# A rotation whose halves are exchanged by transfers of the sine term instead of by a second set of products

## The chip, the core and the metric

The kernel runs on one core of one Trainium2 chip. The metric is the device time of one execution in microseconds (us). Three runs of the kernel before gave a median of 2217.9 us (2217.04 to 2220.73).

## The reference

The program is two transformer layers over 2048 tokens of width 128, in f32. The change lies in the first attention: 16 heads of 64 dimensions, queries and keys made from a latent of 64, and a rotation of all 64 dimensions by the token's place. Cut to what matters:

```python
c_q = h @ w_down_q.T;  c_kv = h @ w_down_kv.T
q = (c_q @ w_up_q.T)  # 16 heads x 64;  k, v from c_kv in the same way
e, o = xr[..., 0::2], xr[..., 1::2]            # even and odd dimensions
rot = stack([e * cos - o * sin, e * sin + o * cos])   # for q and for k
scores = einsum('bhqd,bhkd->bhqk', q, k) / 8
out = softmax(scores) @ v;  out @ w_out.T + residual
```

The first experts, a second attention and second experts follow; the change does not touch them.

## The kernel before

Everything is written out by hand: each engine has its own list of work, sorted by a due time counted in steps, and semaphores join the lists. The function is `heads`. One head has four chunks of 512 queries, one chunk has eight steps of two key tiles, so there are 32 steps to a head and 512 in all.

In a step TensorE (PE) makes two tiles of scores (two 512-column products each, L640 and L641), ScalarE (ACT) writes each tile's exponential twice (f16 at L476, f32 at L477), GpSimd (POOL) subtracts the two for the low half (L428, `low_half`), and PE weighs the values of the step four before with 24 short products (L655 to L659). Between these PE fills the three `aux` banks in PSUM for side work, in the order of `aux_units`: two products a step for the row maxima (L608), which VectorE (DVE) reduces (L533); the shift, the output turn and product; and the rotations.

A rotation ("rope") serves one head's q or k for a pair of chunks, with two chunks on the two halves of the 128 partitions. Each takes two aux units. The first has three products with the weight's columns in even-odd order (`wq`, `wk` and their low halves), the second three with the columns exchanged (`wq_sw`, `wk_sw`). DVE multiplies the first by the cosine (L519), the second by the sine in its bank (L522), and adds the two into `roped` (L527). ACT rounds that to f16 (L464), POOL subtracts for the low half (L422), and SyncE (SP) moves both into the operands: four transfers of the high half (L407), then two of the low half (L413), rotation by rotation. There are 64 rotations: four a head, made during the head before; the first head's stand ahead of the loop, but for its second q rotation, which stands at step 0.

Row maxima of a chunk need the q and k operands in place: the first product for a chunk waits for the high half of q, and those of each key pair for the high and the low half of k. A list's order is fixed, so a wait on one engine holds back everything behind it on that engine.

Ahead of the loop ACT and POOL also split the weights of the later heads (L483 and L435, one instruction per weight on each).

Of the kernel before, what the change touches and what calls it, by code (L numbers as in the profile page):

```python
# [17 lines left out]
P = 128  # L18
# [103 lines left out]

WEIGHTS = ("wq", "wq_sw", "wk", "wk_sw")
FIRST_HEADS = 2 * P
# [175 lines left out]
AUX = 3  # L300
ROPED = 3
STAGED = 2
QRING = 6
PAIRS = NCH // 2
HIGH_MOVES, LOW_MOVES = 4, 2
WEIGHTS_AT = -19
# [4 lines left out]
def rope_at(kind, h, pair):  # L311

    if kind == "k":
        return STEPS * h - (21, 15)[pair] if h else -24 + pair
    return STEPS * h - (27, 5)[pair] if h else (-25, 0)[pair]


def aux_units():

    plan = [(FOLD_AT + 2 * i, "fold", i) for i in range(2)]  # L320
    for h in range(H0):
        for c in range(NCH):
            g, end = NCH * h + c, KPAIR * (NCH * h + c + 1) + LAG
            for kind in "kq" if c % 2 == 0 else "":
                plan += [(rope_at(kind, h, c // 2), "rope", (kind, h, c // 2, part)) for part in range(2)]
# [15 lines left out]
def heads(nc, dram, x, keep):  # L341
    with ExitStack() as ctx:
# [8 lines left out]
        probs_lo = sb("probs_lo", [P, SLOTS, 2, CH], F16)  # L351
        term = [sb(f"rope_term{i}", [P, CH], F32) for i in range(2)]
        roped = [sb(f"roped{i}", [P, CH], F32) for i in range(ROPED)]
        high = [sb(f"rope_high{i}", [P, CH], F16) for i in range(STAGED)]
# [8 lines left out]
        aux = [ps(f"aux{i}", [P, CH], F32) for i in range(AUX)]  # L363
        (aux_full, aux_free, rope_turned, hi_ready, lo_ready, shift_ready, scores_ready, probs_ready, low_ready,
         probs_used, inv_ready, norm_ready, weight_high, weight_ready, xa_full, x_ready) = (
            sem(n) for n in ("aux_full", "aux_free", "rope_turned", "hi_ready", "lo_ready", "shift_ready",
                             "scores_ready", "probs_ready", "low_ready", "probs_used",
                             "inv_ready", "norm_ready", "weight_high",
                             "weight_ready", "xa_full", "x_ready"))
        high_in, low_in = ([sem(f"{n}{i}") for i in range(STAGED)] for n in ("rope_high_in", "rope_low_in"))  # L370
        ident, ident16 = keep["ident"], keep["ident16"]
# [3 lines left out]
        unit_no = {w: n for n, w in enumerate(banked)}  # L375
        ropes = [arg[:3] for kind, arg in banked if kind == "rope" and arg[3] == 0]
        rope_no = {r: n for n, r in enumerate(ropes)}

        def halves_of(kind, h, pair, m):

            c = 2 * pair + m
            if kind == "k":
                a, b, cols = ka[h % 2], kb[h % 2], slice(c * CH, (c + 1) * CH)
            else:
                a, b, cols = qa[(NCH * h + c) % QRING], qb[(NCH * h + c) % QRING], slice(0, CH)
            return a[0:LAT0, cols], a[LAT0:, cols], b[0:LAT0, cols]

        def wait_high(eng, r):
# [7 lines left out]
        with nc.Block() as block:  # L396
            @block.sync
            def _(sp):
                for r, (kind, h, pair) in enumerate(ropes):
                    if r >= STAGED:  # L400
                        wait_high(sp, r - STAGED)
                    sp.wait_ge(hi_ready, r + 1)
                    for m in range(2):
                        a_top, a_bottom, b = halves_of(kind, h, pair, m)
                        rows = high[r % STAGED][m * LAT0:(m + 1) * LAT0, :]
                        for out in (b if kind == "k" else a_top, a_bottom):
                            sp.dma_start(out, rows).then_inc(high_in[r % STAGED], 16)  # L407
                    if r >= STAGED:
                        wait_low(sp, r - STAGED)
                    sp.wait_ge(lo_ready, r + 1)  # L410
                    for m in range(2):
                        a_top, a_bottom, b = halves_of(kind, h, pair, m)
                        sp.dma_start(a_top if kind == "k" else b, low[r % STAGED][m * LAT0:(m + 1) * LAT0, :]  # L413
                                     ).then_inc(low_in[r % STAGED], 16)

            @block.gpsimd
            def _(pool):
                def rope_low(r):
                    pool.wait_ge(hi_ready, r + 1)
                    if r >= STAGED:  # L420
                        wait_low(pool, r - STAGED)
                    pool.tensor_tensor(low[r % STAGED][:], roped[r % ROPED][:], high[r % STAGED][:], ALU.subtract  # L422
                                       ).then_inc(lo_ready, 1)
# [18 lines left out]

                work = [(math.floor(rope_at(*rope)) + 3.5, "rope", r) for r, rope in enumerate(ropes)]
                work += [(n + 1, "low", n) for n in range(ALL)]
# [13 lines left out]
            def _(act):  # L458
                def high_halves(r):
                    act.wait_ge(aux_free, unit_no["rope", (*ropes[r], 1)] + 1)  # L460
# [3 lines left out]
                    act.activation(high[r % STAGED][:], roped[r % ROPED][:], ACT.Copy).then_inc(hi_ready, 1)  # L464

# [26 lines left out]

                work = [(math.floor(rope_at(*rope)) + 2.5, "rope", r) for r, rope in enumerate(ropes)]
                work += [(n, "exp", n) for n in range(ALL)]
# [13 lines left out]
            def _(dve):  # L508
                def empty(kind, arg):
# [4 lines left out]
                    if kind == "rope":  # L514
                        of, h, pair, part = arg
                        r = rope_no[of, h, pair]
                        cols = slice(pair * CH, (pair + 1) * CH)
                        if part == 0:
                            dve.tensor_tensor(term[r % 2][:], bank, keep["cos"][:, cols], ALU.mult  # L519
                                              ).then_inc(aux_free, 1)  # L520
                        else:
                            dve.tensor_tensor(bank, bank, keep["sin"][:, cols], ALU.mult).then_inc(rope_turned, 1)  # L522
                            if r >= ROPED:
                                dve.wait_ge(lo_ready, r - ROPED + 1)
                            dve.wait_ge(aux_free, unit_no["rope", (of, h, pair, 0)] + 1)
                            dve.wait_ge(rope_turned, r + 1)
# [37 lines left out]
                work = [(at, 0, kind, arg) for at, kind, arg in units]  # L564
                work += [(KPAIR * g - 4.9, 1, "reduce", g) for g in range(H0 * NCH)]
                for _, _, kind, arg in sorted(work, key=lambda w: w[:2]):
                    if kind == "reduce":
                        negated_maxima(arg)
                    elif kind == "norm":
                        normalise(arg)  # L570
# [4 lines left out]
            def _(pe):  # L575
                def fill(kind, arg):
# [5 lines left out]
                    if kind == "rope":  # L582
                        of, h, pair, part = arg
                        w = ("wq", "wq_sw", "wk", "wk_sw")[2 * (of == "k") + part]
                        columns, cols = slice(h * P, (h + 1) * P), slice(pair * CH, (pair + 1) * CH)
# [1750 lines left out]
def tables():  # L2336
# [10 lines left out]
    t["cos0"] = by_pair(np.tile(cos, (2, 1)))  # L2347
    t["sin0"] = by_pair(np.concatenate([-sin, sin], 0))

# [32 lines left out]
def layouts(a):  # L2382

    even_odd = np.concatenate([np.arange(0, DH0, 2), np.arange(1, DH0, 2)])
    odd_even = np.concatenate([np.arange(1, DH0, 2), np.arange(0, DH0, 2)])
    twice = lambda w, axis: np.concatenate([w, w], axis)

    def up(w, order):
# [11 lines left out]
        "wq": up(a["L0_attn_w_up_q"], even_odd),  # L2400
        "wq_sw": up(a["L0_attn_w_up_q"], odd_even),
        "wk": up(a["L0_attn_w_up_k"], even_odd),
        "wk_sw": up(a["L0_attn_w_up_k"], odd_even),
        "w_up_v": a["L0_attn_w_up_v"].reshape(H0 // 2, P, LAT0).transpose(1, 0, 2).reshape(P, H0 // 2 * LAT0),
# [48 lines left out]
```

## Time and profile before

| | |
|---|---|
| profiled execution, its own time | 2218.36 us |
| its span, first to last instruction | 2216.5 us |
| mean granted clock of TensorE | 0.935 |
| PE, DVE, ACT, POOL busy in the span | 91%, 76%, 73%, 74% |
| first attention | to about 1260 us of the span |
| transfers, share of 16 engines | 9.2% on the hardware queue |

A busy PE is one whose modelled matmuls overlap, so its share says little of what is left; whether it waits is read from the waits. DVE's and POOL's shares are averages over stages with different limits, and the tables by stretch tell them apart. The attention's loop runs from about 62 us to 1260 us; before it lies a stretch in which the first rotations pass through all engines one after another.

### The profile page before, as it was taken

The numbers are of one execution on the slowest core, as the hardware profiler recorded it, in microseconds if no ns is written. First come the engines' busy times: TensorE is split into PE (matmuls) and PEld (weight loads), VectorE is DVE, ScalarE is ACT, GpSimd is POOL, SyncE is SP. The second block draws the span as 40 slices with busy tenths as digits, with TensorE's granted clock in tenths as the row PEclk, the third lists the DMA queues.
The fourth block names the chain that finished last, engine by engine and source line by source line (L and its number), as shares of the span: only waits on it lengthen the run. The fifth ranks groups of instructions, "written<-read, shape, count | busy, mean of one in ns | idle before, by whom it ended". The sixth has DMA issues, their size and how long they took to land. (4 is left out here: it accounts for less than half of the span.)

```text
span 2216.5 us, 60603 instructions
## 1 busy us (share of the span) xinstructions
PE 2013.8 (91%) x24318; PEld 1318.0 (59%) x24318; DVE 1690.3 (76%) x3487; ACT 1622.9 (73%) x3282; POOL 1630.5 (74%) x1036
## 2 busy tenths in 40 slices
PE   5899999999999999999999989976788887788888
PEld 2466666666666666666666656642456666565665
DVE  5677777777777777777777468968989998899514
ACT  4788898888988989889889846656656565565443
POOL 3699999999999999999999926625663344677600
PEclk8899999999999999999999989978779999998768
DMA  4000100000000000001000001111121111121101
GB/s 152 20 19 23 27 20 23 24 23 23 23 23 23 23 23 23 23 19 28 24 22 18 2 19 27 33 45 26 36 51 36 35 43 38 33 45 39 39 10 38
DMA packets 88224, 67.80 MB, mean 31 GB/s; under 512 B 41280, under 2 KB 78352, under 8 KB 87952
## 3 DMA queue, kind: packets, MB, share of 16 engines
q1 hardware_dynamic: 76432, 52.19, 9.2%
q0 software_dynamic: 11520, 11.82, 2.7%
q8 instruction: 191, 3.13, 0.6%
q14 instruction: 81, 0.66, 0.1%
HBM read 32.97 MB, written 1.61 MB: 16 GB/s over the span
## 5 line engine op out<-in xcount | busy, mean ns | idle before, releaser
L428 POOL TENSOR_TENSOR probs_lo<-probs,probs_hi 128x1024 f16<-128x1024 f32 x512 | 1076.5, 2131 | 65.3 <-ACT probs L477 62.7
L533 DVE TENSOR_REDUCE part_max<-aux 128x1 f32<-128x512 f32 x1024 | 687.8, 687 | 185.6 <-PE aux L608 180.7
L476 ACT ACTIVATE probs_hi<-scores 128x512 f16<-128x512 f32 x1024 | 643.6, 628 | 143.3 <-PE scores L641 116.0
L477 ACT ACTIVATE probs<-scores 128x512 f32<-128x512 f32 x1024 | 649.7, 635 | 0.0
L1732 POOL DMA_INDIRECT far<-key_table,placeT x320 | 326.0, 1019 | 238.3 <-issue 68.6
L655 PE MATMUL acc<-v,probs_hi 128*128 128x65 f16 x4096 | 446.7, 193 | 1.8 <-POOL probs_lo L428 1.8
L657 PE MATMUL acc<-v,probs_hi 128*128 128x64 f16 x4096 | 447.5, 195 | 0.0
L659 PE MATMUL acc<-v,probs_lo 128*128 128x65 f16 x4096 | 445.8, 192 | 0.0
L655 PEld LDWEIGHTS acc<-v,probs_hi 128*128 128x128 f16 x4096 | 382.4, 97 | 73.8 <-POOL probs_lo L428 2.0
L657 PEld LDWEIGHTS acc<-v,probs_hi 128*128 128x128 f16 x4096 | 380.3, 97 | 68.8 <-issue 0.3
L608 PE MATMUL aux<-k_a,q_a 128*128 128x512 f16 x1024 | 393.3, 385 | 13.8 <-DMA k_a<-rope_low 8.5
L640 PE MATMUL scores<-q_a,k_a 128*128 128x512 f16 x1024 | 389.2, 380 | 4.8 <-ACT probs L477 4.7
L641 PE MATMUL scores<-q_b,k_b 65*128 65x512 f16 x1024 | 390.5, 381 | 0.0
L659 PEld LDWEIGHTS acc<-v,probs_lo 128*128 128x128 f16 x4096 | 381.6, 99 | 0.0
L641 PEld LDWEIGHTS scores<-q_b,k_b 65*128 65x128 f16 x1024 | 100.2, 98 | 119.2 <-issue 1.1
L608 PEld LDWEIGHTS aux<-k_a,q_a 128*128 128x128 f16 x1024 | 100.2, 98 | 84.3 <-issue 14.4
L640 PEld LDWEIGHTS scores<-q_a,k_a 128*128 128x128 f16 x1024 | 100.3, 98 | 71.9 <-ACT probs L477 11.8
L1983 PE MATMUL a_turn<-queries,qi 128*128 128x64 f16 x2216 | 83.9, 203 | 40.1 <-DVE qi L1904 39.7
L890 POOL TENSOR_TENSOR e_hid_lo<-e_hid,e_hid_hi 128x512 f16<-128x512 f32 x64 | 74.2, 1160 | 61.4 <-ACT e_hid_hi L842 61.4
L1983 PEld LDWEIGHTS a_turn<-queries,qi 128*128 128x128 f16 x2216 | 79.5, 104 | 46.4 <-issue 41.0
L1757 ACT ACTIVATE far<-a_turn 128x256 f32<-128x256 f32 x34 | 13.0, 383 | 119.3 <-PE a_turn L1983 119.3
L1904 DVE TENSOR_SCALAR qi<-queries,key_id 128x512 f16<-128x512 f16 x277 | 81.5, 363 | 19.8 <-PE a_turn L1983 15.9
(335 smaller groups left out, 3642.0 us busy)
## 6 DMA issues: line engine op xcount, KB each, us to landing
q_a<-rope_high SPq DMA_DIRECT2D x128, 64.0 KB, 2.1
far<-key_table,placeT POOLq DMA_INDIRECT x360, 2.4
q_b<-rope_low SPq DMA_DIRECT2D x64, 64.0 KB, 2.0
k_b<-rope_high SPq DMA_DIRECT2D x64, 64.0 KB, 2.0
k_a<-rope_high SPq DMA_DIRECT2D x64, 64.0 KB, 2.1
k_a<-rope_low SPq DMA_DIRECT2D x64, 64.0 KB, 2.0
qT<-qT SPq DMA_DIRECT2D x16, 256.0 KB
queries<-places SPq DMA_DIRECT2D x7, 512.0 KB, 3.8
```

Source lines behind the costliest of these rows:

```text
L428: pool.tensor_tensor(probs_lo[:, slot], probs[:, wide], probs_hi[:, slot], ALU.subtract).then_inc(low_ready, 1)
L476: act.activation(probs_hi[:, slot, i], bank, ACT.Exp, scale=float(DH0) ** -0.5)
L477: act.activation(probs[:, wide, i], bank, ACT.Exp, scale=float(DH0) ** -0.5).then_inc(probs_ready, 1)
L533: dve.tensor_reduce(part_max[g % 2][:, n % QT, n // QT:n // QT + 1], bank, AX.X, ALU.max).then_inc(aux_free, 1)
L608: ins = pe.matmul(bank, qa[g % QRING][:, t * P:(t + 1) * P], ka[h % 2][:, c * CH:(c + 1) * CH], start=True, stop=True)
L640: pe.matmul(out, ka[h % 2][:, keys], qa[g % QRING][:], start=True, stop=False)
L641: pe.matmul(out, kb[h % 2][:, keys], qb[g % QRING][:], start=False, stop=True).then_inc(scores_ready, 1)
L655: pe.matmul(out, probs_hi[:, n % SLOTS, i, queries], high, start=(kt == 0 and t == 0), stop=False, skip_group_check=True)
L657: pe.matmul(out[:, 0:DH0], probs_hi[:, n % SLOTS, i, queries], low, start=False, stop=False, skip_group_check=True)
L659: ins = pe.matmul(out, probs_lo[:, n % SLOTS, i, queries], high, start=False, stop=(kt == KT0 - 1), skip_group_check=True)
L1732: pool.indirect_dma_start(far[m][:, i, :], None, keep["table"], bass.IndirectOffsetOnAxis(ap=place_of(placeT, t, i), axis=0)).then_inc(far ...
L1983: ins = pe.matmul(b[:, i * KW:(i + 1) * KW], hot_tile(t, k, kt)[:, i * P:(i + 1) * P], split[:, kt, part * KW:(part + 1) * KW], start=(kt ...
```

## The change

The second set of products goes. From one bank DVE makes two products in SBUF, `turned` = bank x sine and `term` = bank x cosine. SP copies the four 32-row halves of `turned` crosswise into `swapped`, and DVE later adds `swapped` to `term` (`join`). The sine table's signs are exchanged to fit. ACT and POOL read `term` where they read `roped`. SP's list is now sorted by due time, with swaps, high moves and low moves of different rotations interleaved. All due times of the rotations are new, and the first head's second q rotation stands ahead of the loop. The two exchanged weights are no longer loaded or split.

```diff
-WEIGHTS = ("wq", "wq_sw", "wk", "wk_sw")
+WEIGHTS = ("wq", "wk")
-ROPED = 3
+TERMS = 4
+HALF0 = LAT0 // 2
+SWAPS, HIGH_MOVES, LOW_MOVES = 4, 4, 2
+JOIN_AFTER, HIGH_AFTER, LOW_AFTER = 3.5, 4.5, 5.5
 def rope_at(kind, h, pair):
     if kind == "k":
-        return STEPS * h - (21, 15)[pair] if h else -24 + pair
-    return STEPS * h - (27, 5)[pair] if h else (-25, 0)[pair]
+        return STEPS * h - (23, 18)[pair] if h else (-26, -25.4)[pair]
+    return STEPS * h - (29, 7)[pair] if h else (-25.7, -20)[pair]
...
+                def swap_halves(r):
+                    sp.wait_ge(aux_free, unit_no["rope", ropes[r]] + 1)
+                    if r >= STAGED:
+                        wait_swapped(sp, r - STAGED)
+                    if r >= TERMS:
+                        sp.wait_ge(roped_ready, r - TERMS + 1)
+                    for m in range(2):
+                        for part in range(2):
+                            src = m * LAT0 + part * HALF0
+                            dst = m * LAT0 + (1 - part) * HALF0
+                            sp.dma_start(swapped[r % TERMS][dst:dst + HALF0, :], turned[r % TERMS][src:src + HALF0, :]
+                                         ).then_inc(swap_in[r % STAGED], 16)
...
+                work = [(rope_at(*rope) + 1, swap_halves, r) for r, rope in enumerate(ropes)]
+                work += [(rope_at(*rope) + HIGH_AFTER + 0.5, move_high, r) for r, rope in enumerate(ropes)]
+                work += [(rope_at(*rope) + LOW_AFTER + 0.5, move_low, r) for r, rope in enumerate(ropes)]
+                for _, move, r in sorted(work, key=lambda w: w[0]):
+                    move(r)
...
-                            dve.tensor_tensor(term[r % 2][:], bank, keep["cos"][:, cols], ALU.mult
-                                              ).then_inc(aux_free, 1)
...
-                            dve.tensor_tensor(bank, bank, keep["sin"][:, cols], ALU.mult).then_inc(rope_turned, 1)
...
-                            dve.tensor_tensor(roped[r % ROPED][:], bank, term[r % 2][:], ALU.add
-                                              ).then_inc(aux_free, 1)
+                        dve.tensor_tensor(turned[r % TERMS][:], bank, keep["sin"][:, cols], ALU.mult)
+                        dve.tensor_tensor(term[r % TERMS][:], bank, keep["cos"][:, cols], ALU.mult).then_inc(aux_free, 1)
...
+                def join(r):
+                    out = term[r % TERMS][:]
+                    dve.wait_ge(aux_free, unit_no["rope", ropes[r]] + 1)
+                    wait_swapped(dve, r)
+                    dve.tensor_tensor(out, out, swapped[r % TERMS][:], ALU.add).then_inc(roped_ready, 1)
```

SP's list at the start, before: each rotation's four high moves and two low moves stand together (`rope_high`, `rope_low` are the staged halves, `q_a`, `q_b`, `k_a`, `k_b` the operands).

```order
L407 DMA q_a<-rope_high 64x512 x4
L413 DMA q_b<-rope_low 64x512 x2
L407 DMA k_b<-rope_high 64x512
L407 DMA k_a<-rope_high 64x512
L407 DMA k_b<-rope_high 64x512
L407 DMA k_a<-rope_high 64x512
L413 DMA k_a<-rope_low 64x512 x2
```

The same list now, from the first swap to the fourth (buffer numbers shown).

```order
L418 DMA rope_swapped0<-rope_turned0 32x512 x4
L418 DMA rope_swapped1<-rope_turned1 32x512 x4
L418 DMA rope_swapped2<-rope_turned2 32x512 x4
L431 DMA k_b0<-rope_high0 64x512
...
L431 DMA q_a1<-rope_high1 64x512 x2
...
L431 DMA k_a0<-rope_high0 64x512
L441 DMA k_a0<-rope_low0 64x512 x2
L441 DMA q_b0<-rope_low1 64x512
L441 DMA q_b1<-rope_low1 64x512
L441 DMA k_a0<-rope_low0 64x512 x2
L418 DMA rope_swapped3<-rope_turned3 32x512 x4
```

The first low move, third in its own rotation before, now stands behind three swaps and three sets of high moves, and the fourth swap behind three sets of low moves.

DVE's list at the start, before: the third rotation, then the first row maxima.

```order
L519 TENSOR_TENSOR rope_term0<-aux1,cos 128x512
L522 TENSOR_TENSOR aux2<-aux2,sin 128x512
L527 TENSOR_TENSOR roped2<-aux2,rope_term0 128x512
L533 TENSOR_REDUCE part_max0<-aux0 128x1
```

DVE's list at the same place now, from the second rotation's cosine on.

```order
L554 TENSOR_TENSOR rope_term1<-aux1,cos 128x512
L553 TENSOR_TENSOR rope_turned2<-aux2,sin 128x512
L554 TENSOR_TENSOR rope_term2<-aux2,cos 128x512
L577 TENSOR_TENSOR rope_term0<-rope_term0,rope_swapped0 128x512
L577 TENSOR_TENSOR rope_term1<-rope_term1,rope_swapped1 128x512
L577 TENSOR_TENSOR rope_term2<-rope_term2,rope_swapped2 128x512
L553 TENSOR_TENSOR rope_turned3<-aux0,sin 128x512
L554 TENSOR_TENSOR rope_term3<-aux0,cos 128x512
L577 TENSOR_TENSOR rope_term3<-rope_term3,rope_swapped3 128x512
L559 TENSOR_REDUCE part_max0<-aux1 128x1
```

The first row maximum now stands behind four joins, the last of which waits for the fourth swap.

## Rows read from the trace of the kernel before

**Rows 1.** Busy us by stretch, heads 1 to 14: one pair of heads, then all seven.
```profile
753.20:903.00 149.80, 149.80 (x2050) 97.04 (x2049) 116.68 (x192) 133.78 (x265) 143.28 (x74) 1.00 0.09 23
...
sum 1048.20, PE 1047.84 PEld 678.66 DVE 816.39 ACT 935.55 POOL 1002.35; mean PE 149.69 PEld 96.95 DVE 116.63 ACT 133.65 POOL 143.19
```

**Rows 2.** Waits in heads 1 to 14: us in total, times, longest.
```profile
POOL probs_lo L428 <- ACT probs L477: 43.3, 63, 1.7
...
PE aux L608 <- DMA k_a<-rope_low: 0.3, 1, 0.3
```

**Rows 3.** POOL's groups in heads 1 to 14: count, busy, mean ns, idle before.
```profile
L428 POOL TENSOR_TENSOR probs_lo<-probs,probs_hi 128x1024 f16<-128x1024 f32 x449 | 944.3, 2131 | 45.8 <-ACT probs L477 43.3
L422 POOL TENSOR_TENSOR rope_low<-roped,rope_high 128x512 f16<-128x512 f32 x56 | 64.8, 1157 | 0.0
```

**Rows 4.** PE in order of time: a step with a rotation, then a plain one.
```profile
759.71 0.38 PE L640 MATMUL scores<-q_a,k_a 128*128 128x512 f16 x1
...
760.80 0.38 PE L589 MATMUL aux<-cq,wq 128*128 128x512 f16 x1
...
763.05 0.38 PE L640 MATMUL scores<-q_a,k_a 128*128 128x512 f16 x1
...
765.09 0.38 PE L640 MATMUL scores<-q_a,k_a 128*128 128x512 f16 x1
```

**Rows 5.** DVE's groups by form, after the first attention: an add of two SBUF tensors.
```profile
L1144 DVE TENSOR_TENSOR far<-far_turned,far_swapped 128x512 f32<-128x512 f32 x31 | 21.4, 692 | 1.1
```

**Rows 6.** DVE in order of time, first experts: operations on two SBUF tensors.
```profile
1300.91 0.42 DVE L978 TENSOR_TENSOR gate_chosen<-gate_hit,group_mask 128x256 f32<-128x256 f32 x1
...
1307.66 1.35 DVE L922 TENSOR_TENSOR gate_chosen<-gate_chosen,gate_hit 128x256 f32<-128x256 f32 x1
...
1309.50 0.42 DVE L922 TENSOR_TENSOR gate_chosen<-gate_chosen,gate_hit 128x256 f32<-128x256 f32 x1
```

**Rows 7.** POOL in the same stretch.
```profile
1301.06 1.30 POOL L890 TENSOR_TENSOR e_hid_lo<-e_hid,e_hid_hi 128x512 f16<-128x512 f32 x1 [7.30 <-ACT e_hid_hi L842]
1303.16 1.16 POOL L890 TENSOR_TENSOR e_hid_lo<-e_hid,e_hid_hi 128x512 f16<-128x512 f32 x1 [0.81 <-ACT e_hid_hi L842]
...
1307.58 1.15 POOL L890 TENSOR_TENSOR e_hid_lo<-e_hid,e_hid_hi 128x512 f16<-128x512 f32 x1 [2.39 <-ACT e_hid_hi L842]
```

**Rows 8.** All engines in order of time, ahead of the loop.
```profile
33.61 0.69 DVE L519 TENSOR_TENSOR rope_term<-aux,cos 128x512 f32<-128x512 f32 x1 [1.88 <-PE aux L591]
...
37.00 2.45 SPq L407 DMA_DIRECT2D q_a<-rope_high  x4
...
39.49 1.23 SPq L413 DMA_DIRECT2D q_b<-rope_low  x2
...
42.33 1.15 POOL L422 TENSOR_TENSOR rope_low<-roped,rope_high 128x512 f16<-128x512 f32 x1 [2.13 <-DMA q_b<-rope_low]
...
43.44 3.58 POOL L435 TENSOR_TENSOR wq_lo<-w_stage,wq 128x1792 f16<-128x1792 f32 x1
...
46.73 9.65 DVE L533 TENSOR_REDUCE part_max<-aux 128x1 f32<-128x512 f32 x16 [6.42 <-PE aux L608]
```

**Rows 9.** Transfers: KB each, median us from issue to landing.
```profile
q_a<-rope_high SPq DMA_DIRECT2D x128, 64.0 KB, 2.1
```

**Rows 10.** PE in order of time, the loop's first steps (L640 begins a tile).
```profile
61.48 0.63 PE L640 MATMUL scores<-q_a,k_a 128*128 128x512 f16 x1
61.90 0.63 PE L641 MATMUL scores<-q_b,k_b 65*128 65x512 f16 x1
...
75.47 0.59 PE L608 MATMUL aux<-k_a,q_a 128*128 128x512 f16 x1 [4.60 <-issue]
75.86 0.63 PE L640 MATMUL scores<-q_a,k_a 128*128 128x512 f16 x1
...
80.04 0.38 PE L640 MATMUL scores<-q_a,k_a 128*128 128x512 f16 x1
```

More of the change, by code:

```diff
@@ L324, in aux_units @@
             for kind in "kq" if c % 2 == 0 else "":
-                plan += [(rope_at(kind, h, c // 2), "rope", (kind, h, c // 2, part)) for part in range(2)]
+                plan += [(rope_at(kind, h, c // 2), "rope", (kind, h, c // 2))]
             plan += [(KPAIR * g - 12.5 + n / 2, "max", (g, n)) for n in range(NCH * QT)]
@@ L351, in heads @@
         probs_lo = sb("probs_lo", [P, SLOTS, 2, CH], F16)
-        term = [sb(f"rope_term{i}", [P, CH], F32) for i in range(2)]
-        roped = [sb(f"roped{i}", [P, CH], F32) for i in range(ROPED)]
+        term = [sb(f"rope_term{i}", [P, CH], F32) for i in range(TERMS)]
+        turned = [sb(f"rope_turned{i}", [P, CH], F32) for i in range(TERMS)]
+        swapped = [sb(f"rope_swapped{i}", [P, CH], F32) for i in range(TERMS)]
         high = [sb(f"rope_high{i}", [P, CH], F16) for i in range(STAGED)]
@@ L369, in heads @@
                              "weight_ready", "xa_full", "x_ready"))
+        swap_in = [sem(f"rope_swap_in{i}") for i in range(STAGED)]
         high_in, low_in = ([sem(f"{n}{i}") for i in range(STAGED)] for n in ("rope_high_in", "rope_low_in"))
@@ L375, in heads @@
         unit_no = {w: n for n, w in enumerate(banked)}
-        ropes = [arg[:3] for kind, arg in banked if kind == "rope" and arg[3] == 0]
+        ropes = [arg for kind, arg in banked if kind == "rope"]
         rope_no = {r: n for n, r in enumerate(ropes)}
@@ L398, in _, with move_high @@
             def _(sp):
-                for r, (kind, h, pair) in enumerate(ropes):
+                def swap_halves(r):
[10 more added lines that the diff above has]
+                                         ).then_inc(swap_in[r % STAGED], 16)
+                def move_high(r):
+                    kind, h, pair = ropes[r]
                     if r >= STAGED:
@@ L407, in _, with move_low @@
                             sp.dma_start(out, rows).then_inc(high_in[r % STAGED], 16)
+                def move_low(r):
+                    kind, h, pair = ropes[r]
                     if r >= STAGED:
@@ L421, in rope_low @@
                         wait_low(pool, r - STAGED)
-                    pool.tensor_tensor(low[r % STAGED][:], roped[r % ROPED][:], high[r % STAGED][:], ALU.subtract
+                    pool.tensor_tensor(low[r % STAGED][:], term[r % TERMS][:], high[r % STAGED][:], ALU.subtract
                                        ).then_inc(lo_ready, 1)
@@ L441, in residual @@
                     pool.tensor_tensor(x[:], x[:], keep["xa"][:], ALU.add).then_inc(x_ready, 1)
-                work = [(math.floor(rope_at(*rope)) + 3.5, "rope", r) for r, rope in enumerate(ropes)]
+                work = [(rope_at(*rope) + LOW_AFTER, "rope", r) for r, rope in enumerate(ropes)]
                 work += [(n + 1, "low", n) for n in range(ALL)]
@@ L459, in high_halves @@
                 def high_halves(r):
-                    act.wait_ge(aux_free, unit_no["rope", (*ropes[r], 1)] + 1)
+                    act.wait_ge(roped_ready, r + 1)
                     if r >= STAGED:
@@ L463, in high_halves @@
                         act.wait_ge(lo_ready, r - STAGED + 1)
-                    act.activation(high[r % STAGED][:], roped[r % ROPED][:], ACT.Copy).then_inc(hi_ready, 1)
+                    act.activation(high[r % STAGED][:], term[r % TERMS][:], ACT.Copy).then_inc(hi_ready, 1)
                 def exponentials(n):
@@ L491, in normed @@
                         ins.then_inc(xa_full, 1)
-                work = [(math.floor(rope_at(*rope)) + 2.5, "rope", r) for r, rope in enumerate(ropes)]
+                work = [(rope_at(*rope) + HIGH_AFTER, "rope", r) for r, rope in enumerate(ropes)]
                 work += [(n, "exp", n) for n in range(ALL)]
@@ L565, in _ @@
                 work += [(KPAIR * g - 4.9, 1, "reduce", g) for g in range(H0 * NCH)]
+                work += [(rope_at(*rope) + JOIN_AFTER, 2, "join", r) for r, rope in enumerate(ropes)]
                 for _, _, kind, arg in sorted(work, key=lambda w: w[:2]):
@@ L568, in _ @@
                         negated_maxima(arg)
+                    elif kind == "join":
+                        join(arg)
                     elif kind == "norm":
@@ L582, in fill @@
                     if kind == "rope":
[L583 to L584 removed]
+                        of, h, pair = arg
+                        w = "w" + of
                         columns, cols = slice(h * P, (h + 1) * P), slice(pair * CH, (pair + 1) * CH)
```

23 lines of the change are left out of this document (8 added, 15 removed).

## The prediction

> **What bounds the kernel now.** I read the busy times by stretch first, since the page's shares average over stages. Heads 1 to 14 take 1048.2 us, 149.7 to a pair of heads, and in them PE is busy for 1047.84 and POOL for 1002.35 [rows 1]. PE's busy time is modelled, so I then read the waits: PE waits there for a transfer for 0.3 us and for no other engine as much, while POOL waits 43.3 us for ACT, in 63 short waits [rows 2]. PE therefore sets the pace; POOL, with its 449 low halves and 56 low halves of rotations, is second with some 45.8 us to spare [rows 3], which is 4%. Third I read PE in order of time: a plain step takes 763.05 to 765.09, 2.04 us, one with a rotation 759.71 to 763.05, 3.34; the difference, 1.30, is its six products at 0.217 each [rows 4].
>
> The stretch ahead of the loop is bound otherwise. Rotations pass through DVE, ACT, POOL and SP in turn; the first row maximum is reduced at 46.73 [rows 8], the first scores begin at 61.48, and at 75.47 PE has stood still for 4.60 us [rows 10]. Its second q rotation stands at step 0, and PE reaches the maxima that need it before its transfers have landed.
>
> **The products in the loop.** Three of six products go: 56 x 3 x 0.217 = 36.4 us. PE would need 1047.8 - 36.4 = 1011.4 us for heads 1 to 14. Nothing hides PE's work, so this would be the gain if nobody else were late. Next is POOL at 1002.35 as it stands, so what POOL loses or gains decides.
>
> **The join.** DVE has three operations of a rotation before and three now, all over 512 columns; the one kind of that form in the trace, an add of two SBUF tensors, takes 692 ns [rows 5], so DVE's own work stays. What is new is where it reads. Before, each operation took at most one tensor from SBUF and the other from a PSUM bank; the join takes both from SBUF. The first experts show what such an operation does beside POOL. One on 256 columns takes 0.42 us, but the one that began at 1307.66 took 1.35 and ended at 1309.01, 0.28 after the POOL operation that ran from 1307.58 to 1308.73 [rows 6, 7]. The other way round, one began on DVE at 1300.91, and the POOL operation begun at 1301.06 took 1.30 where its like takes 1.16: it was held 0.14, until 0.29 after DVE's start [rows 6, 7]. So the two exclude each other, and POOL loses about 0.29 us to one on 256 columns. For 512 I add (0.692 - 0.42), the price of 256 more columns: 0.56.
>
> POOL runs its work almost without a gap, so nearly every join meets it. POOL then needs 1002.35 + 56 x 0.56 = 1033.7 us, above PE's 1011.4, and becomes the bound. The gain in heads 1 to 14 is 1048.2 - 1033.7 = 14.5 us instead of 36.4. The ends of the price are 0 (joins that fall into POOL's gaps) and 4.1 (the second rival); I take the value of the two events, since they are the same two engines in the same kind of operation.
>
> The Trainium skill ("SBUF - State Buffer", section "Who interferes with whom") says that a DVE instruction with two SBUF inputs contends with a GpSimd instruction that reads SBUF, and that whichever issues first holds the shared read interface for its whole instruction. The trace agrees on the exclusion; on how long, its 0.29 of 0.42 us is less than the whole. By the page's whole instruction, 0.69 each, POOL would need 1041.1 and the gain would be 7.1.
>
> The join also waits, for POOL's running operation (0 to 2.1 us, 1.0 on average) and for its swap. Behind it on DVE stand the row maxima, and for those PE waits once its three aux banks are full. A swap is four issues, 2.45 us, with the last landing 2.1 after its issue [rows 8, 9]: about 4 us, against 3.5 steps or 7.1 us until the join is due. That cover shrinks when SP is late. The swap of a head's first k rotation stands on SP one due step behind the low move of the q rotation before it, and that waits for POOL. When POOL is the slow engine this holds up DVE and then PE; PE now has 22 us to spare in the 14 heads, and a PE that waits lets POOL catch up, so I count 2 us for all of it (0 at best; at worst PE's spare is used up and 9 come on top).
>
> **The start.** Here the change makes a chain longer. The first DVE product would still begin at 33.61 [rows 8]; two products of 0.69 that start 0.6 apart (as 16 maxima take 9.65), and `aux_free` comes at about 34.95. SP issues three swaps at 2.45 each, to 42.3. Then two sets of high moves, to 47.2, and the third, to 49.65. Only then the first low move, which before stood third: issues to 50.9, landed about 52.3. POOL's third low half waits for that landing, as it did at 42.33 [rows 8], and ends at 53.5; its move is out at 54.75, the fourth swap at 57.2, landed at 58.65. The fourth join waits for that and the first row maximum stands behind it: 59.35 at best. POOL has its two weights in hand (3.58 each [rows 8], 53.5 to 60.6), so by the exclusion above the join ends at about 60.9. Against 46.73 the maxima begin 12.6 to 14.2 late, and with them the first scores, at about 75.7 for 61.48.
>
> Part of this comes back. Before, the first four steps took 61.48 to 75.86, 14.4 us, with the second q rotation and the 4.60 stall in them [rows 10]; both are gone. Two steps at half rate (six products at 0.43, 2.6) and two at ACT's pace (935.55 us in 448 steps, about 2.0 [rows 1]) make 9.2: 5.2 back. The step begun at 75.86 ran 4.18 at half rate after that stall [rows 10]; without the stall I count 1.7 back. Four rotations at 0.65 give 2.6. So 9.5 of 14.2 return, and the start and head 0 cost 4.7 (3 to 9: less if the port is free for the fourth join, more if head 0's four joins are not covered by POOL's waits there).
>
> Head 15 makes no rotation and does not change. Two weights fewer to load and split lie beside the start's chain and count nothing; they shorten POOL's queue ahead of the fourth join, which is in the 60.6.
>
> **The sum.** 2218.4 (the profiled execution) - 14.5 + 4.7 + 2 = 2210.6. That execution stands 0.5 above the median, so 2210.
>
> **Rivals.**
> - *The joins cost POOL nothing worth naming.* POOL's 45.8 us of gaps [rows 3] speak for it, and that the evidence is two events on shorter operations; against it, the gaps are short and 96% of POOL's time has none. PE then sets the pace: 2218.4 - 36.4 + 2 + 3.5 = 2187. Between it and the forecast the time moves with the price, from 0.16 us a join (where POOL and PE tie) up.
> - *Slower: POOL loses more than 0.73 us to a join.* That is the point of decision: (45.85 - 4.7) / 56. Mechanism: while POOL's operations follow each other without a gap, the join does not get in until POOL runs dry; DVE's maxima stand behind it, PE's aux banks fill, no scores come, and POOL idles until the join (0.69), a maximum (0.60), PE (0.65) and ACT's two tiles (2.1) have run: up to 4.1 us each. For it: no event in the trace has POOL with a second operation queued behind the first. Against it: in the one event with POOL first, DVE went on 0.28 us after POOL's end. At 1.0 us a join, some of them held up, the time is 2218.4 + 10.2 + 4.7 = 2233; if every join is held, 56 x 4.1 + 1002 gives about 2400.
> - *The start is not won back.* If head 0's steps are slow for another reason (the weights' and the residual's work on ACT and POOL), 14.2 stays and eats the gain: 2218.4 - 14.5 + 14.2 + 2 = 2220.
>
> **How the numbers follow.** From no change I tell apart 0.2%, 4.4 us: faster is under 2213.5, slower over 2222.3. The forecast (price 0.45 to 0.70, 2204 to 2218) has 0.50, of which 0.41 is faster and 0.09 the same; free joins have 0.17, all faster; the start not won back has 0.11, the same; POOL losing more than 0.73 has 0.22, slower. Faster 0.58, same 0.20, slower 0.22. The range goes from 2188, where little but the free joins' best is left out, to 2233, beyond which about half of the slow rival lies. The forecast's own range is 2204 to 2218.
>
> **What would show it.** In the profile after: plain steps paced by POOL at about 2.1 us instead of 2.04, with PE's waits for ACT's scores and POOL's busy time near its span in heads 1 to 14; low halves of 2.13 us stretched to about 2.7 where a join runs; joins of 1 to 3 us where 0.69 is their own; the first row maximum at 59 to 61 us; no stall of 4.6 in the loop's first steps. I am wrong if a pair of heads takes under 146 us (free joins), over 149.7 (joins held up), or if the first maximum comes before 55.

## The result, and the profile after

The changed kernel takes 2242.4 us, the median of four runs (2236.6 to 2247.2), against 2217.8 before: a ratio of 1.0107 (1.0086 to 1.0128). It is slower by 1.1%, where 2210 was forecast, and above the forecast's range.

Four stretches of the profiled executions (2218.36 before, 2244.16 after) say where the 25.8 us are. Except for the outer ends, each begins and ends at the first score of a head.

| stretch | before | after | difference | forecast |
|---|---|---|---|---|
| to the first score | 61.48 | 76.42 | +14.9 | +14.2 |
| head 0 | 88.1 | 84.4 | -3.7 | -9.5 |
| heads 1 to 14 | 1048.8 | 1062.9 | +14.1 | -12.5 |
| head 15 and all that follows | | | +0.5 | 0 |

The loss is in the start, as forecast, and in heads 1 to 14, the long stretch, from which a gain was forecast. The busy times there, a pair of heads to a row, by POOL's heads as in [rows 1] (columns: stretch, its length, then PE, PEld, DVE, ACT and POOL with counts, granted clock, DMA share, GB/s):

```profile
315.30:464.10 148.80, 147.55 (x2062) 96.14 (x2061) 122.37 (x195) 136.41 (x268) 146.62 (x73) 1.00 0.15 37
464.10:616.60 152.50, 147.13 (x2029) 94.93 (x2026) 126.41 (x192) 134.72 (x265) 145.83 (x73) 0.99 0.15 36
616.60:769.80 153.20, 148.05 (x2032) 95.52 (x2029) 126.51 (x192) 134.81 (x265) 145.93 (x74) 0.98 0.15 36
...
sum 1062.40, PE 1030.04 PEld 667.16 DVE 878.85 ACT 943.03 POOL 1022.99; mean PE 147.15 PEld 95.31 DVE 125.55 ACT 134.72 POOL 146.14
```

POOL is busy for 1022.99, less than the 1033.7 that was forecast, and yet a pair of heads takes 148.8 to 153.4 instead of 149.7 before (the prediction had named anything over 149.7 as its sign of joins held up). So POOL, the busiest engine but PE, does not set this time by its work. The waits of the same stretch say who does (us in total, times, longest), and POOL's groups how its operations changed (count; busy, mean ns; idle before), to be held against [rows 2, 3]:

```profile
ACT rope_high L498 <- DVE rope_term L577: 38.3, 24, 4.5
PEld aux L644 <- DVE part_max L559: 34.6, 19, 4.0
POOL probs_lo L462 <- ACT probs L511: 31.0, 60, 2.1
PE aux L644 <- DVE part_max L559: 28.1, 16, 3.9
...
POOL rope_low L456 <- ACT rope_high L498: 9.0, 7, 1.3
```

```profile
L462 POOL TENSOR_TENSOR probs_lo<-probs,probs_hi 128x1024 f16<-128x1024 f32 x448 | 962.1, 2178 | 31.2 <-ACT probs L511 31.0
L456 POOL TENSOR_TENSOR rope_low<-rope_term,rope_high 128x512 f16<-128x512 f32 x56 | 64.6, 1153 | 9.0 <-ACT rope_high L498 9.0
```

PE and ACT wait for DVE, up to 4.5 us at a time; before, PE's waits for DVE came to 2.1 us in the whole stretch, none above 0.4. The DVE line that both lead back to is the join, L577 (`rope_term` is `term`; the columns give count and shortest/median/longest in ns):

```profile
L577 DVE TENSOR_TENSOR rope_term<-rope_term,rope_swapped x56: 680/1458/6432, 177.6 to 1213.4; 128x512 f32<-128x512 f32 x56
its engine sat idle before it (us, times) until:
  DMA rope_swapped<-rope_turned: 0.5, 1
```

The swaps are in time: one wait of 0.5 us in 14 heads. But an operation whose shortest is 0.68 us lasts up to 6.43. Of all 64 joins 17 last under 0.8 us, 19 under 1.6, 20 under 3, and eight 5.00 to 6.43. These eight are another kind, as one of each, 151 us apart, shows in order of time (start, duration, engine; a row of POOL with x3 is three operations without a gap):

```profile
301.05 6.30 POOL L462 TENSOR_TENSOR probs_lo<-probs,probs_hi 128x1024 f16<-128x1024 f32 x3
302.16 5.74 DVE L577 TENSOR_TENSOR rope_term<-rope_term,rope_swapped 128x512 f32<-128x512 f32 x1
307.82 1.27 DVE L559 TENSOR_REDUCE part_max<-aux 128x1 f32<-128x512 f32 x2
307.93 0.63 ACT L498 ACTIVATE rope_high<-rope_term 128x512 f16<-128x512 f32 x1 [3.93 <-DVE rope_term L577]
308.55 0.41 PE L644 MATMUL aux<-k_a,q_a 128*128 128x512 f16 x1 [3.31 <-DVE part_max L559]
308.63 1.15 POOL L456 TENSOR_TENSOR rope_low<-rope_term,rope_high 128x512 f16<-128x512 f32 x1 [1.29 <-ACT rope_high L498]
...
452.09 4.66 POOL L462 TENSOR_TENSOR probs_lo<-probs,probs_hi 128x1024 f16<-128x1024 f32 x2
453.19 1.57 DVE L577 TENSOR_TENSOR rope_term<-rope_term,rope_swapped 128x512 f32<-128x512 f32 x1
```

Both joins come 1.1 us after POOL has begun an operation. At 453.19 the join gets in when that operation ends: the join ends at 454.76, and POOL's next operation is stretched (two in 4.66 us where the lost turn's three take 6.30, 2.10 each). At 302.16 POOL runs three operations in 6.30 us, unstretched; the join ends at 307.90, 0.55 after the last of the three, when POOL has nothing left. Meanwhile everything stops in a ring: DVE's maxima stand behind the join, PE behind the maxima, ACT's `rope_high` stands on the join with the exponentials behind it, and POOL runs dry for want of exponentials. The join gets in when POOL has run dry, and not before.

A long join costs PE once more, by its clock. After the one at 474.95 (6.43 us) PE's first product waits 3.87 us; in the stretches around it the column behind POOL is the granted clock:

```profile
482.04 0.39 PE L644 MATMUL aux<-k_a,q_a 128*128 128x512 f16 x1 [3.87 <-DVE part_max L559]
```

```profile
474.00:482.00 8.00, 4.17 (x63) 2.61 (x59) 7.74 (x5) 3.50 (x8) 6.83 (x4) 1.00 0.00 0
482.00:486.00 4.00, 3.75 (x21) 1.75 (x22) 2.47 (x4) 3.95 (x9) 3.08 (x2) 0.61 0.28 69
486.00:490.00 4.00, 4.00 (x51) 2.30 (x49) 3.18 (x5) 2.42 (x5) 2.56 (x3) 0.96 0.27 67
```

PE stood still, and in the next 4 us ran mostly at the lower level of 1.2 GHz. PE's busy time in the long stretch is 1030.0 us, where 1011.4 was forecast, but not all of that is the clock: with POOL's waits (below) it is still 1021.3 at a granted clock of 1.00. The other 8.8 us may be the clock's; that split was not tested.

The start went as forecast (DVE's and POOL's rows, then PE's first score; [rows 8, 10] before):

```profile
57.65 3.57 POOL L469 TENSOR_TENSOR wk_lo<-w_stage,wk 128x1792 f16<-128x1792 f32 x1
...
59.42 2.34 DVE L577 TENSOR_TENSOR rope_term<-rope_term,rope_swapped 128x512 f32<-128x512 f32 x1 [13.55 <-DMA rope_swapped<-rope_turned]
61.69 1.27 DVE L559 TENSOR_REDUCE part_max<-aux 128x1 f32<-128x512 f32 x2
...
76.42 0.64 PE L676 MATMUL scores<-q_a,k_a 128*128 128x512 f16 x1
```

The fourth join began at 59.42 and ended at 61.76, 0.54 after POOL's second weight (61.22).

### The profile page after: what moved, and what is told of

It reads as the page before. It is cut to its first block and busy times, and to the rows that moved or that the text cites. A ratio compares the mean times of both kernels' runs of the same rounds, so it can differ in the third digit from the quotient of the medians.

```text
span 2242.4 us, 60583 instructions
## 1 busy us (share of the span) xinstructions
PE 1985.2 (89%) x24126; PEld 1304.1 (58%) x24126; DVE 1760.9 (79%) x3487; ACT 1626.4 (73%) x3278; POOL 1646.3 (73%) x1032
## 5 line engine op out<-in xcount | busy, mean ns | idle before, releaser
L462 POOL TENSOR_TENSOR probs_lo<-probs,probs_hi 128x1024 f16<-128x1024 f32 x512 | 1097.2, 2174 | 53.9 <-ACT probs L511 53.6
L510 ACT ACTIVATE probs_hi<-scores 128x512 f16<-128x512 f32 x1024 | 628.7, 614 | 104.6 <-PE scores L677 93.9
L511 ACT ACTIVATE probs<-scores 128x512 f32<-128x512 f32 x1024 | 634.7, 620 | 0.0
L693 PE MATMUL acc<-v,probs_hi 128*128 128x64 f16 x4096 | 452.2, 196 | 0.0
L676 PE MATMUL scores<-q_a,k_a 128*128 128x512 f16 x1024 | 394.1, 385 | 7.7 <-ACT probs L511 7.5
L676 PEld LDWEIGHTS scores<-q_a,k_a 128*128 128x128 f16 x1024 | 100.9, 99 | 82.1 <-ACT probs L511 24.1
L577 DVE TENSOR_TENSOR rope_term<-rope_term,rope_swapped 128x512 f32<-128x512 f32 x64 | 130.0, 2031 | 19.4 <-DMA rope_swapped<-rope_turned 19.4
L2019 PE MATMUL a_turn<-queries,qi 128*128 128x64 f16 x2216 | 89.7, 210 | 38.9 <-DVE qi L1940 38.8
L2019 PEld LDWEIGHTS a_turn<-queries,qi 128*128 128x128 f16 x2216 | 85.8, 109 | 44.8 <-issue 39.8
L456 POOL TENSOR_TENSOR rope_low<-rope_term,rope_high 128x512 f16<-128x512 f32 x64 | 73.8, 1154 | 41.3 <-ACT rope_high L498 32.2
```

The source lines that it names most:

```text
L462: pool.tensor_tensor(probs_lo[:, slot], probs[:, wide], probs_hi[:, slot], ALU.subtract).then_inc(low_ready, 1)
L510: act.activation(probs_hi[:, slot, i], bank, ACT.Exp, scale=float(DH0) ** -0.5)
L511: act.activation(probs[:, wide, i], bank, ACT.Exp, scale=float(DH0) ** -0.5).then_inc(probs_ready, 1)
L676: pe.matmul(out, ka[h % 2][:, keys], qa[g % QRING][:], start=True, stop=False)
L693: pe.matmul(out[:, 0:DH0], probs_hi[:, n % SLOTS, i, queries], low, start=False, stop=False, skip_group_check=True)
L2019: ins = pe.matmul(b[:, i * KW:(i + 1) * KW], hot_tile(t, k, kt)[:, i * P:(i + 1) * P], split[:, kt, part * KW:(part + 1) * KW], start=(kt ...
```

## The experiments

The theory (theory 1 where a text numbers them): what costs is that the join reads two SBUF tensors beside a POOL that never pauses, and of that mostly the joins that lose their turn. The rival: the new chain (swap by transfers, join, high half, low half) is too long for its due times, or costs in another way. Times behind "Measured" are medians, and ratios go against the kernel before, timed beside each run on the same chip; times of stretches and operations are those of one profiled execution of each kernel.

**One SBUF input.** The join copies `swapped` alone, so the cosine term is left out of the result; order, waits and transfers stay.

```diff
-dve.tensor_tensor(out, out, swapped[r % TERMS][:], ALU.add).then_inc(roped_ready, 1)
+dve.tensor_reduce(out, swapped[r % TERMS][:].unsqueeze(2), AX.X, ALU.max).then_inc(roped_ready, 1)
```

> The changed kernel whose join reads one SBUF tensor alone (it copies the swapped sine term by a reduction over one element, and so leaves the cosine term out of the rotation); its place, its waits and its columns stay. Theory 1, lost turns: the join and POOL's subtractions exclude each other; a join that gets its turn costs POOL some 0.45 us, and one that loses its turn holds DVE for 5 to 6 us until POOL runs dry. Then all joins take about 0.69 us here, POOL's subtractions 2.13, heads 1 to 14 go from 1062.4 to 1012 to 1020 us, and the time is 2187 to 2197. Theory 2, the long chain: the swap, the join and the moves arrive too late for the lists of DVE, ACT and POOL as they are placed, whatever the join reads. Then the time stays at 2235 to 2247.

Measured: 2186.0 us, ratio 0.986 (0.984 to 0.988), a little under the range of theory 1. All joins are alike, POOL's operations are not stretched, and PE works through heads 1 to 14 (here from its first score of head 1 to 0.4 us before that of head 15) without a gap:

```profile
L577 DVE TENSOR_REDUCE rope_term<-rope_swapped x55: 674/676/677, 168.4 to 1134.9; 128x512 f32<-128x512 f32 x55
```

```profile
L462 POOL TENSOR_TENSOR probs_lo<-probs,probs_hi 128x1024 f16<-128x1024 f32 x449 | 942.8, 2137 | 11.1 <-ACT probs L511 10.4
```

```profile
151.78:1163.80 1012.02, 1011.81 (x14163) 662.12 (x14162) 808.91 (x1344) 940.24 (x1849) 1000.88 (x505) 1.00 0.16 38
```

The chain with its transfers is the same and costs nothing in heads 1 to 14; at the start it still does, since the first score comes at 73.62 for 61.48 before. Reading the second SBUF input costs 56 us (2242.4 - 2186.0), more than twice what the change lost. The operation changes too, from an add to a reduction; the run with POOL's waits, below, keeps the add. PE's 1011.81 is close to the forecast's 1011.4.

**The kernel before, its add with two SBUF inputs.** The sine product goes to SBUF instead of back to its bank; no swap, six products as before.

```diff
-dve.tensor_tensor(bank, bank, keep["sin"][:, cols], ALU.mult).then_inc(rope_turned, 1)
+dve.tensor_tensor(turned[r % 2][:], bank, keep["sin"][:, cols], ALU.mult).then_inc(rope_turned, 1)
-dve.tensor_tensor(roped[r % ROPED][:], bank, term[r % 2][:], ALU.add
+dve.tensor_tensor(roped[r % ROPED][:], turned[r % 2][:], term[r % 2][:], ALU.add
```

> The kernel before with one operand changed: DVE writes the sine product to SBUF instead of back into its bank, so that the add that follows reads two SBUF tensors, as the join does. No swap, all products, all due times as before. Theory 1, lost turns: POOL has 45.8 us to spare in heads 1 to 14 and PE sets the pace, so adds that get their turn (0.45 us of POOL each) cost nothing, and what is lost is lost by the adds that lose their turn: some adds of over 3 us appear, and the time is 2222 to 2243. Theory 2, the long chain: no change, 2217 to 2219.

Measured: 2293.7, ratio 1.0345 (1.0317 to 1.0373). The direction is the theory's, the size was far off: the add is longer, 5.47 or 5.48 us in five of 64 and 2.89 to 3.05 in three more, and PE waits for it:

```profile
L529 DVE TENSOR_TENSOR roped<-rope_turned,rope_term x56: 762/1808/5484, 164.1 to 1252.4; 128x512 f32<-128x512 f32 x56
...
  PEld aux L615: 42.8, 22
  PEld aux L610: 17.1, 20
  PE aux L610: 12.1, 20
```

In the kernel before, the same add took 0.69 each time. Here the add itself frees an aux bank, for which PE's maxima wait (L610), and behind 22 of the adds PE waits for its bank and for the shift reduction that stands right behind the add (L615), so that adds of 2 us, too, make PE wait. Heads 1 to 14 take 1117.8, 69 us more than before. What a wait costs depends on what is queued behind it; the size can't be carried from one order of work to another.

**POOL waits for the join.** From the fifth rotation on, POOL's list waits for `roped_ready` at the join's due time.

```diff
+work += [(rope_at(*rope) + JOIN_AFTER, "join", r) for r, rope in enumerate(ropes) if r >= 4]
...
+elif kind == "join":
+    pool.wait_ge(roped_ready, n + 1)
```

> The changed kernel with one wait more: from the fifth rotation on POOL's list has, at the join's own due time, a wait until the join is done, so that no subtraction stands behind the running one while a join wants in. Theory 1, lost turns: no join in the loop takes over 3 us; each costs POOL 0.5 to 0.8 us, heads 1 to 14 take 1036 to 1050, and the time is 2217 to 2232. Theory 2, the long chain: POOL now waits for it too, and the time is 2245 or more.

Measured: 2214.9, ratio 0.999 (0.998 to 1.000): no different from the kernel before, and a little better than theory 1 had it (2217 to 2232). A wait that is added takes 27.5 us away from the changed kernel. No join of the loop is longer than 2.69 us, heads 1 to 14 take 1035.9 (the forecast, 1033.7), and the granted clock stays at 1.00:

```profile
154.40:1190.30 1035.90, 1021.27 (x14169) 656.86 (x14168) 858.30 (x1344) 944.27 (x1849) 1000.68 (x505) 1.00 0.15 38
```

```profile
POOL probs_lo L462 <- DVE rope_term L580: 30.8, 49, 0.6
```

```profile
L462 POOL TENSOR_TENSOR probs_lo<-probs,probs_hi 128x1024 f16<-128x1024 f32 x449 | 942.8, 2133 | 35.2 <-DVE rope_term L580 30.8 <-ACT probs L514 4.4
```

POOL pays 0.6 us for each of 49 joins, by standing still instead of by being stretched (mean 2133 ns). Head 0 takes 78.7: 9.4 less than before, the forecast's 9.5.

**The high half later.** ACT's and POOL's halves of a rotation are due one step later in the changed kernel, so ACT has two more tiles ahead of its wait for the join.

```diff
-JOIN_AFTER, HIGH_AFTER, LOW_AFTER = 3.5, 4.5, 5.5
+JOIN_AFTER, HIGH_AFTER, LOW_AFTER = 3.5, 5.5, 6.5
```

> The changed kernel with ACT's high half and POOL's low half of a rotation due one step later (5.5 and 6.5 steps behind its products instead of 4.5 and 5.5); joins stay at 3.5. Theory (lost turns: a join that misses its turn gets in only when POOL has no operation ready, which comes about because ACT's high half stands on the join and writes no exponentials): with ACT free for two more tiles POOL runs dry later, so the joins that lose their turn last longer, 6.5 to 9 us instead of 5.0 to 6.4, and the time is 2242 or more. Rival (the chain swap, join, high half, low half is simply too tight, and ACT's 38 us of waits are its price): the waits of ACT for joins go and the time falls to 2225 to 2235.

Measured: 2256.1 (2235.8 to 2266.8), ratio 1.015 (1.010 to 1.020). The theory's joins came: again eight long ones, now 7.26 to 8.51 us.

```profile
L577 DVE TENSOR_TENSOR rope_term<-rope_term,rope_swapped x64: 680/1328/8505, 37.0 to 1222.1; 128x512 f32<-128x512 f32 x64
```

Heads 1 to 14 take 1087.5 for 1062.9. A looser chain made it worse: a join that lost its turn lasts until POOL has nothing to do, and POOL had one operation more.

**The fourth join behind the first maxima.**

```diff
-work += [(rope_at(*rope) + JOIN_AFTER, 2, "join", r) for r, rope in enumerate(ropes)]
+work += [(rope_at(*rope) + JOIN_AFTER + 12.5 * (r == 3), 2, "join", r) for r, rope in enumerate(ropes)]
```

> The changed kernel with the first head's fourth join due 12.5 steps later on DVE, so that the first row maxima stand ahead of it; nothing else moves. If the start is long because the first maxima stand behind the fourth join, the first maximum is reduced at about 53 us instead of 61.69, the first scores come about 8.7 earlier, and the time is 2233 to 2236. Rival: head 0 takes the gain back (its maxima and its second q rotation are late in another way): 2240 to 2244.

Measured: 2238.9 (2237.7 to 2241.3), ratio 1.0087 (1.0067 to 1.0108).

```profile
52.10 1.29 DVE L559 TENSOR_REDUCE part_max<-aux 128x1 f32<-128x512 f32 x2 [7.76 <-PE aux L644]
...
67.45 0.63 PE L676 MATMUL scores<-q_a,k_a 128*128 128x512 f16 x1
```

The first maximum comes 9.6 us earlier, the first score 9.0, and head 0 keeps its 84.3. The attention ends 9.3 earlier in the profiled execution, but what follows took 3.8 longer there, and the medians differ by 3.4, less than the 6 to 9 expected; their ranges overlap. The 2238.9 lies between the two ranges expected, 2233 to 2236 and 2240 to 2244, so the time settles nothing; the rows show that the start did get shorter.

**Both edits.** POOL's waits and the late fourth join together.

```diff
+work += [(rope_at(*rope) + JOIN_AFTER, "join", r) for r, rope in enumerate(ropes) if r >= 4]
...
+work += [(rope_at(*rope) + JOIN_AFTER + 12.5 * (r == 3), 2, "join", r) for r, rope in enumerate(ropes)]
```

> Two edits together: POOL's list waits for each join at the join's due time (from the fifth rotation on, as in the run with POOL's waits), and the first head's fourth join stands behind the first row maxima. The first edit alone gave 2214.9; if the second is worth 6 to 9 beside it, 2206 to 2209, faster than the kernel before (2217). If the start's gain is taken back in head 0, 2214 to 2216.

Measured: 2206.1 (2204.2 to 2213.0), ratio 0.9945 (0.9927 to 0.9963): 0.55% faster than the kernel before, the best that leaves nothing out. The three runs that follow start from this one.

**POOL's wait half a step later.**

```diff
-(rope_at(*rope) + JOIN_AFTER, "join", r)
+(rope_at(*rope) + JOIN_AFTER + 0.5, "join", r)
```

> As the run with POOL's waits and the fourth join late, but POOL's wait stands half a step later in its list, behind one more low half. Theory (a join that gets its turn holds POOL 0.45 us, one that loses it waits until POOL is made to stop): most joins get their turn beside the extra low half and POOL then passes its wait at once; the others are bounded by one low half more (joins up to 4.8 us). POOL's cost per join falls from about 0.6 to about 0.5 us: 2200 to 2207. Rival: the extra low half always runs ahead of the join, so that all joins take 2.1 us longer and DVE and ACT get late: 2212 to 2225.

Measured: 2207.3, ratio 0.9944 (0.9927 to 0.9962). The edit left every list as it was: the wait still sorted ahead of the low half due at the same time. It tells nothing of the theory; it is the same program again, and repeats to 1.2 us of the median.

**POOL's wait one step later**, now truly behind one more low half.

```diff
-(rope_at(*rope) + JOIN_AFTER, "join", r)
+(rope_at(*rope) + JOIN_AFTER + 1.0, "join", r)
```

> As the run with POOL's waits and the fourth join late, but POOL's wait stands one step later in its list, behind one more low half (half a step later had left the list as it was). If a join that comes while POOL runs usually gets its turn and holds POOL 0.45 us, POOL mostly finds its wait already met, and those that lose their turn last one low half longer, up to 4.8 us: 2200 to 2207. Rival: a queued low half mostly runs ahead of the join, so that joins get 2.1 us longer and DVE, PE and ACT are late: 2212 to 2225.

Measured: 2214.0 (2207.9 to 2217.8), ratio 0.9973 (0.9958 to 0.9988).

```profile
L580 DVE TENSOR_TENSOR rope_term<-rope_term,rope_swapped x56: 679/1693/4342, 166.2 to 1182.5; 128x512 f32<-128x512 f32 x56
```

The theory's bound on the joins came out: eight last 3.86 to 4.34 us, and four more that let one operation pass 2.90 to 2.93. The time did not: it lies in the rival's range (2212 to 2225), though the rival's mechanism did not come, since 48 of the 60 joins got their turn. The gain in POOL's cost did not pay for the other twelve.

**POOL waits for few.** Only for the joins with number 7 and 0 of each eight, where seven of the changed kernel's eight long ones are.

```diff
-... if r >= 4]
+... if r >= 4 and r % 8 in (7, 0)]
```

> As the run with POOL's waits and the fourth join late, but POOL waits only for the joins with number 7 and 0 of each eight (15 of 60), which are those that took 5 us or more in the changed kernel. If the long joins are the loss and the others cost POOL the 0.45 us by which they stretch its operation, no join is over 3 us and the time is 2200 to 2208, about that with all waits. Rival: losing the turn is a matter of how far POOL and DVE have drifted, so that other joins lose it instead: some joins of 5 us or more, and 2212 to 2240.

Measured: 2230.3 (2226.0 to 2235.1), ratio 1.0055 (1.0032 to 1.0077). The rival of this run holds. Numbers 7 and 0 are cured, and number 3 of each eight, harmless in the changed kernel but for one, now takes 5.00 or 5.01 us, seven times:

```profile
L580 DVE TENSOR_TENSOR rope_term<-rope_term,rope_swapped x56: 679/1976/5010, 163.5 to 1202.3; 128x512 f32<-128x512 f32 x56
```

So losing the turn belongs to no join in particular.

**The kernel before, its second q rotation early.** The change's plan for the first head (-20 instead of step 0) without the change.

```diff
-    return STEPS * h - (27, 5)[pair] if h else (-25, 0)[pair]
+    return STEPS * h - (27, 5)[pair] if h else (-25, -20)[pair]
```

> The kernel before with one due time changed: the first head's second q rotation stands ahead of the loop, as in the changed kernel. If the 4.60 us for which PE stands still in the loop's first steps and the half rate behind it come from that rotation's late transfers, the stall is gone, the first row maximum stays at about 46.7 and the time falls to 2209 to 2213. If something else (ACT's pace in those steps) takes it back, it stays at 2216 to 2219.

Measured: 2211.8, ratio 0.997 (0.9955 to 0.9986). Head 0 falls from 88.1 to 80.5:

```profile
61.36:141.82 80.46, 75.67 (x938) 44.22 (x937) 57.54 (x94) 71.45 (x147) 71.44 (x35) 0.97 0.08 19
```

Most of what head 0 gives back is owed to this one number, and the kernel before could have had it. Against this kernel the best of the changed ones is ahead by 0.25% only (0.9945 to 0.997), and the two intervals overlap.

Read together, the runs on the changed kernel's chain form a scale of the longest joins in heads 1 to 14 (one profiled execution each):

| run | long joins there | their length | heads 1 to 14 |
|---|---|---|---|
| one SBUF input | none | 0.68 | 1012.4 |
| both edits | none | to 2.68 | 1035.8 |
| wait one step later | 7 | 3.86 to 4.34 | 1039.7 |
| POOL waits for few | 7 | 5.01 | 1061.1 |
| changed kernel | 7 | 5.00 to 6.43 | 1062.9 |
| high half later | 8 | 7.26 to 8.51 | 1087.5 |

Above the second row, a join of 5 us costs (1061.1 - 1035.8) / 7 = 3.6 us, one of the changed kernel (1062.9 - 1035.8) / 7 = 3.9, one of 8 us (1087.5 - 1035.8) / 8 = 6.5. These are estimates: they put the whole difference on the long joins, though the others cost POOL 0.6 us where it waits and 0.45 where it does not. One of about 4 us comes to 0.6 by the same sum, but that it costs so little is not shown: the execution behind that row took 2208.5 where the median is 2214.0, and its head 0, with one join of 4.22 us, took 82.1 where both edits have 78.7.

## Why the prediction was wrong, point by point

- **Products.** Right: with one SBUF input PE needs 1011.8 for heads 1 to 14, 1011.4 was worked out, and the rival of free joins (2187) gives that run's time, 2186.0.
- **The join's price.** This step failed: "so nearly every join meets it", at 0.56 each, for all. For a join that gets its turn the price was good: 49 of POOL's operations in heads 1 to 14 are stretched, from 2.13 to a median of 2.58, so 0.45. But one in eight does not get it, and waits 5 to 6.4 us with the other engines behind it. The step took a price from two events in the first experts, where no second POOL operation was ready behind the first; one of its own rivals had named that gap in the evidence. With 56 x 0.56 = 31.4 forecast and 26.6 us above the forecast in the table, a join cost 1.04 us on average, and the rival's point of decision was 0.73.
- **The slower rival's mechanism** was the right one, in its order: the join waits until POOL runs dry, maxima, aux banks, scores, POOL idle. Its price of up to 4.1 us for a held join is close to the 3.9 estimated above, in part by luck: it counted POOL's idle time, and around the join at 302.16 POOL idles for only 2.1 us (1.29 ahead of the rotation's low half, 0.79 behind it). The rival had a chance of 0.22, and the range ended at its first time, 2233, 9 us short of the measured one.
- **DVE's and SP's waits.** 2 us were counted for late swaps; the trace has one of 0.5. With POOL waiting, heads 1 to 14 take 1035.9 against 1033.7 + 2, in part by luck: POOL there stands still for 30.8 us instead of being stretched by 31.4.
- **The start.** The chain was right: first maximum 61.69 for 60.9, first score 76.42 for 75.7, and moving the fourth join gave 9.6 us back. "9.5 of 14.2 return" was right for a head without a long join (9.4 with POOL waiting); in the changed kernel 3.7 returned, as the eighth rotation's join took 6.28 us in head 0's last steps. (Head 0 takes 84.3 or 84.4 in the two runs of the new chain with such a join there, and 77.8 to 78.7 in the six where that join lasts 2.12 us or less.)
- **The sum.** 2210.6 + 26.6 (heads 1 to 14: +14.1 for -12.5) + 6.6 (start and head 0: 11.3 for 4.7) + 0.5 (the rest) = 2244.3; the profiled execution took 2244.16.

By the Trainium skill ("SBUF - State Buffer", section "SBUF: two separate sides") whichever instruction starts first has the shared pair of ports for its whole length and the other blocks. The trace agrees that they exclude each other, but differs on the price: POOL lost 0.45 us to a join of 0.69, and this measured price is the one to use here. A blocked join stayed out over as many as three POOL operations here, on which that sentence says nothing.

One condition can be read from the traces: whether POOL's next subtraction already had its exponentials when the join came. In the changed kernel 18 of the loop's 60 joins came before that, and none lost its turn; all eight that lost it are among the other 42. The runs with the high half later, the late fourth join and the two inputs in the kernel before agree: 0 of 64 against 24 of 116 let at least one more whole operation of POOL pass. With POOL's waits, which keep the next operation back, none is long.

What stays open is which of the joins that meet a ready operation lose their turn. The two shown above came at the same place in POOL's operation (1.11 and 1.10 us in), both with the next operation's input ready 0.62 us earlier; one got in and one did not. Neither the place nor the readiness tells them apart.

## What to carry to other kernels

An operation with two SBUF inputs on DVE, beside a POOL that runs without a gap, had no fair turn in this case: count such a one twice, once as a stretch of POOL's operation, and once as the chance that all that stands behind it waits until POOL runs dry. If it can't read one input from PSUM, make the saturated engine wait for it at its due time; that small, known wait was 27 us cheaper here. And when a price is taken from a few events, ask whether in them the other engine had its next operation ready.

## What had not been expected of the hardware

A join that misses its turn lets up to three POOL operations of 2.1 us pass in the changed kernel, and four with the high half later, though it has waited since the first. The whole stall looks like slack in every sum of busy times: POOL's 1022.99 in 1062.4 is 96%, as before. And a wait of POOL for each join, put in front of an operation, shortened the program by 1.2%.
